# Moving the small stages of an attention and mixture-of-experts block to other half-steps of a hand-placed schedule

## The reference, cut to what matters

```python
q = (x @ Wq.T + bq) ...; k = ...; v = ...
q = _apply_rope(q, cos, sin); k = _apply_rope(k, cos, sin)
attn = softmax(einsum('bhsd,bhed->bhse', q, k) * scale)
x = x + (einsum('bhse,bhed->bhsd', attn, v) ... @ Wo.T + bo)
normed = rms_norm(layernorm(x).astype(bf16)) * norm_weight
scores, idx = top_k(normed @ gate_weight.T + gate_bias, 2); combine = softmax weights of the two
p1 = einsum('bsh,eoh->bseo', normed, mlp1_weight); act = g * sigmoid(1.702 * g) * (lin + 1)
x = x + xc + sum over e of combine[e] * (act @ mlp2_weight[e])
```

## Time and profile before

| | |
|---|---|
| median of 3 runs | 1128.25 us (1126.47 to 1128.8) |
| the profiled execution | 1125.54 us, of which the span from first to last instruction is 1123.7 us |
| PE busy | 953.0 us (85%), 5288 instructions |
| DVE busy | 822.6 us (73%), 1641 instructions |
| ACT busy | 694.7 us (62%), 905 instructions |
| POOL busy | 427.2 us (38%), 356 instructions |
| mean granted TensorE clock | 0.938 of full speed |

### The profile page before, as it was taken

The page is one execution under the profiler, slowest core; times in us unless marked ns, Lnnn a source line. Parts: engine busy times, 40 slices in busy tenths (PEclk is TensorE's granted clock), DMA queues, the critical chain, the costliest instruction groups (busy, mean ns, idle before and its releaser), DMA issues.

```text
span 1123.7 us, 16639 instructions
## 1 busy us (share of the span) xinstructions
PE 953.0 (85%) x5288; PEld 400.6 (36%) x5288; DVE 822.6 (73%) x1641; ACT 694.7 (62%) x905; POOL 427.2 (38%) x356
## 2 busy tenths in 40 slices
PE   4629999889888998989989898989999999995564
PEld 1302222234342443334442343324443443343343
DVE  5751211589968898589958898588968996997897
ACT  2317887766657675766658575766668777760231
POOL 2413302534364334543354434543342332333242
PEclk9868999999999999999999999999999999996686
DMA  5353434344545244444534244444534454331110
GB/s 162 97 120 69 114 82 115 81 104 110 114 90 137 72 105 109 109 101 103 124 82 117 82 108 106 104 91 114 124 82 114 105 123 97 89 91 38 42 57 24
DMA packets 79987, 109.81 MB, mean 98 GB/s; under 512 B 22530, under 2 KB 56722, under 8 KB 76818
## 3 DMA queue, kind: packets, MB, share of 16 engines
q1 hardware_dynamic: 61460, 83.47, 32.5%
q10 hardware_dynamic: 18432, 25.17, 7.7%
HBM read 82.90 MB, written 25.69 MB: 97 GB/s over the span
## 4 chain that ended last, share of the span: by engine, by line
PE 49%; DVE 27%; issue 8%; ACT 6%; POOL 3%; DMA 3%; SPq 2%; ACTq 0%; DVEq 0%; POOLq 0%
PE OP L698 14%; PE S L684 13%; PE D L670 7%; ACT probs L815 4%; DVE act_sb L1123 4%; DVE th_sb L1118 4%; DVE acc L1113 3%; PE A L653 3%; DVE l_sb L1103 3%; PE D L574 3%; DVE g_sb L1101 3%; PE BB L653 3%; PE D L596 3%; DMA o_scr<-O 1%; PE D L588 1%
## 5 line engine op out<-in xcount | busy, mean ns | idle before, releaser
L815 ACT ACTIVATE probs<-S 128x1024 f32<-128x1024 f32 x512 | 511.4, 1022 | 200.4 <-PE S L684 196.7
L684 PE MATMUL S<-Qs,Ks 98*128 98x512 bf16 x1024 | 304.2, 390 | 30.3 <-DMA Qs<-m_scr 15.2
L698 PE MATMUL OP<-probs,V 128*17 128x512 f32 x2048 | 276.4, 612 | 3.0 <-ACT O L824 3.0
L899 POOL TENSOR_TENSOR act_lo<-act_sb,act_hi 128x512 fp32r<-128x512 f32 x128 | 166.3, 1300 | 197.3 <-DVE act_hi L1129 160.8
L684 PEld LDWEIGHTS S<-Qs,Ks 98*128 98x128 bf16 x1024 | 80.3, 99 | 213.8 <-ACT probs L815 95.0
L670 PE MATMUL D<-W,act_hi 128*128 128x256 f32 x448 | 131.6, 326 | 14.0 <-DVE Vn L997 5.8
L1113 DVE SCALAR_TENSOR_TENSOR acc<-D,combh,acc 128x256 f32<-128x256 f32 x224 | 97.1, 475 | 45.8 <-PE D L670 45.6
L1118 DVE SCALAR_TENSOR_TENSOR th_sb<-th_sb,g_sb 128x512 f32<-128x512 f32 x128 | 126.8, 991 | 0.2
L893 POOL TENSOR_SCALAR W<-W2b 128x512 fp32r<-128x512 bf16 x64 | 46.1, 720 | 204.8 <-PE D L670 199.7
L670 PE MATMUL D<-W,act_lo 128*128 128x256 f32 x448 | 112.7, 284 | 0.0
L1123 DVE SCALAR_TENSOR_TENSOR act_sb<-l_sb,th_sb 128x512 f32<-128x512 f32 x128 | 106.0, 828 | 4.4
(11 more groups left out here) (138 smaller groups left out, 991.7 us busy)
## 6 DMA issues: line engine op xcount, KB each, us to landing
W<-in_w ACTq DMA_DIRECT2D x64, 256.0 KB, 2.9
Ks<-k_scr SPq DMA_DIRECT2D x32, 384.0 KB
W2b<-in_w ACTq DMA_DIRECT2D x64, 128.0 KB, 3.1
Ks<-k_scr SPq DMA_DIRECT2D x32, 256.0 KB
o_scr<-O SPq DMA_DIRECT2D x32, 256.0 KB, 4.7
q_scr<-parts SPq DMA_DIRECT2D x16, 384.0 KB, 3.5
k_scr<-parts SPq DMA_DIRECT2D x16, 384.0 KB, 2.5
Qs<-q_scr SPq DMA_DIRECT2D x32, 192.0 KB
```

The costliest lines, as they stand in the source:

```text
L684: last = mm(S[:, j2, C * i:C * (i + 1)], Ks[0:SROWS + MROWS, g % 2, j, P * kt:P * (kt + 1)], Qs[0:SROWS + MROWS, g % 2, j, :], start=True, ...
L698: last = mm(OP[32 * j:32 * j + VW, :], V[:, kt, HG * g + j, :], probs[:, s % 2, C * j:C * (j + 1)], start=kt == 0, stop=kt == KT - 1)
L815: nc.scalar.activation(probs[:, s % 2, 2 * C * j2:2 * C * (j2 + 1)], S[:, j2, :], ACT.Exp, scale=SCALE).then_inc(exp_done, 1)
L899: tt(act_lo[:, e % 2, it, :], act_sb[:, a % 2, :], act_hi[:, e % 2, it, :].bitcast(FP32), ALU.subtract).then_inc(lo_s, 1)
```

## The change

The table `AT` of places is rewritten, and `length` is split: POOL's subtraction becomes a stage `r1` of its own, five halves behind `qk` as it was, and `length` (PE and DVE) gets a place of its own for each block, as have `gmax`, `guard` and `flag`. No operation is added or taken out; only places, and with them the order in each engine's queue, change. In half-steps, before and after:

| stage | before | after |
|---|---|---|
| x_next | 8 | 10 |
| xT1 | 8 | 9 |
| qk0, qk1, qk2, qk3 | 10, 12, 22, 30 | 19, 21, 30, 34 |
| rope, part1, r1, part2, part3 (behind qk) | +2, +3, +5, +7, +10 | the same |
| length0 to length3 | 15, 17, 27, 35 | 24, 26, 35, 41 |
| v0, v1 | 37, 42 | 43, 49 |
| gmax, guard, flag | 36, 39, 41 | 42, 45, 47 |
| wo1 | 14 | 15 |
| stats2, rstd2, xc | 15, 16, 17 | 16, 17, 18 |
| ss, ms, rrms | 18, 18, 20 | 19, 20, 21 |
| nf, nfT | 22, 24 | 23, 25 |
| logits, gates1, etop, gates2 | 26, 26, 27, 28 | 27, 27, 28, 29 |
| combT, b20, b21 | 32, 33, 34 | 31, 33, 36 |

```diff
-    AT = {"x_next": 8, "stats1": 1, "rstd1": 1, "xn": 4, "xT0": 7, "xT1": 8, "qk0": 10, "qk1": 12, "qk2": 22,
-          "qk3": 30, "rope": 2, "part1": 3, "length": 5, "part2": 7, "part3": 10, "v0": 37, "v1": 42, "gmax": 1,
-          "guard": 4, "flag": 6, "x1_in": 0, "x1_b": 11, "wo0": 13, "wo1": 14, "stats2": 15, "rstd2": 16, "xc": 17, "ss":
-          18, "ms": 18, "rrms": 20, "nf": 22, "nfT": 24, "logits": 26, "gates1": 26, "etop": 27, "gates2": 28,
-          "combT": 32, "b20": 33, "b21": 34}
+    AT = {"x_next": 10, "stats1": 1, "rstd1": 1, "xn": 4, "xT0": 7, "xT1": 9, "qk0": 19, "qk1": 21, "qk2": 30, "qk3":
+          34, "rope": 2, "part1": 3, "r1": 5, "part2": 7, "part3": 10, "length0": 24, "length1": 26,
+          "length2": 35, "length3": 41, "v0": 43, "v1": 49, "gmax": 42, "guard": 45, "flag": 47, "x1_in": 0,
+          "x1_b": 11, "wo0": 13, "wo1": 15, "stats2": 16, "rstd2": 17, "xc": 18, "ss": 19, "ms": 20, "rrms":
+          21, "nf": 23, "nfT": 25, "logits": 27, "gates1": 27, "etop": 28, "gates2": 29, "combT": 31, "b20":
+          33, "b21": 36}
...
         place(PREP, h, ("qk", a))
-        for st in ("rope", "part1", "length", "part2", "part3"):
+        place(PREP, AT[f"length{a}"], ("length", a))
+        for st in ("rope", "part1", "r1", "part2", "part3"):
             place(PREP, h + AT[st], (st, a))
     for st in ("gmax", "guard", "flag"):
-        place(PREP, h + AT["length"] + AT[st], (st, 0))
+        place(PREP, AT[st], (st, 0))
...
-            HEAD += [("length", *tile[2]), ("part2", *tile[2]), ("part3", *tile[2])]
+            HEAD += [("r1", *tile[2]), ("length", *tile[2]), ("part2", *tile[2]), ("part3", *tile[2])]
...
-                elif st == "length":
+                elif st == "r1":
                     pool.wait_ge(qk_p1, 4 * u + a + 1)
                     tt(sw[:, a % 2, :], rot[:, a % 2, :], parts[:, a % 2, 0, :], ALU.subtract).then_inc(qk_r1, 1)
```

## The result

The changed kernel takes 1225.75 us (median of 4 runs, 1213.64 to 1228.42) beside 1128.53 us for the kernel before (4 runs): a ratio of 1.0845 (95% interval 1.0769 to 1.0920), 97 us slower. Slower was forecast, but by 24 us and not by 97, and the time lies far above the range. The profiled execution took 1223.82 us with a span of 1222.0 us, 98.3 more than the span before. In the code after, the lines named in the front have two added (L574 is L576, L1113 is L1115).

A forecast was written before the change was run, and what follows sets the result against it. No engine alone: ACT bounds steps 10 to 13, PE and DVE near limit in 14 to 25. Per full window -7.6 + 7.8 + 4.8 = +5.0, four times; window 1 +5.3, tail -1: +24, 1150 us, range 1110 to 1170.

The forecast's parts named there:

- Steps 4 to 9 (-7.6): Two qk products, length0, length1 and their waits leave: 33.8 to 26.2 us per full window, bounds -8.5 and -6.5.
- the 2.9 foretold: Steps 5 and 6 of window 3 should each be shorter by 2.9 us, with no wait for acc.
- the 1.7 foretold: Steps 8 and 9: length0 and length1, with the waits of the down behind them, leave, saving 1.7 us.
- two exchanges that were put at nothing: xT1 ahead of step 5's down, wo1 ahead of step 8's: each makes and saves a wait, together nothing.
- Steps 10 to 13 (+7.8): The first two blocks' chain to length1, woven with POST's norm, takes 19.4 us for 11.6; bounds +6.1 and +10.
- Steps 14 to 25 (+4.8): 2.8 us of added DVE work plus two of four POOL collisions at 1.0 each; bounds -2 and +7.
- two added waits: up 1 waits for g_sb behind 14 small DVE operations; qk3 waits for b20's copy; both counted inside +4.8.
- the gain at `wo1` and `b21` stands against `gates1`: Windows 6 and 7, POST alone: gain and loss offset, so put at nothing.
- the gain foretold for `final`: Tail: final of window 6 runs ahead of ms on DVE while ACT does ss, about -1 us.
- (a): Rival: PE bounds steps 14 to 25 and bank waits go, so faster, 1107 us; chance 0.19.
- (b): Rival: long PE waits bring a lower clock, +7.5 to +15 us more, 1157 to 1165 us; chance 0.25.
- (c): Rival: steps 4 to 13 cancel and steps 14 to 25 hide what comes, 1126 us; chance 0.08.

The follow-up runs named there:

- e1: Changed kernel with POST (wo1 to b21) back at its old places, so PREP's moves alone; 1185.2 us, ratio 1.0532.
- e2: Kernel before with all of POST (wo1 to b21) at its new places and nothing else moved; 1188.0 us, ratio 1.0545.
- e11: Changed kernel with qk1 at half-step 26 for 21 and length1 at 32 for 26; 1236.4 us, ratio 1.0983.
- e12: Changed kernel with length0 at half-step 23 for 24, so its maximum stands ahead of nf on DVE; 1227.6 us, ratio 1.0903.
- e6: Kernel before with qk2, qk3 and their followers (length2, length3, v0, v1, gmax, guard, flag) at their new half-steps; 1163.4 us, ratio 1.0343.
- e3: Changed kernel with logits, gates1, etop and gates2 back at half-steps 26, 26, 27, 28; 1202.7 us, ratio 1.0678.
- e4: Changed kernel with qk0, qk1, length0 and length1 and what follows them back at their old half-steps; 1210.9 us, ratio 1.0747.
- e10: Changed kernel with extra overwritten products on PE, two before combT's wait and three ahead of nfT's bank wait; 1220.3 us, ratio 1.0823.
- e8: Changed kernel with combT at half-step 33 for 31 and b20 at 34 for 33; 1229.4 us, ratio 1.0877.
- e13: Changed kernel with length3 at half-step 42 for 41; 1225.3 us, ratio 1.0838.
- e15: Kernel before with b21 alone moved, to half-step 36 for 34; 1136.1 us, ratio 1.0074.

## Why the prediction was wrong, and where it held

**Steps 4 to 9 (-7.6).** Right in the mechanism: -6.4 on the mean of the four full windows, just outside the upper bound of -6.5. The `qk`'s wait for `acc` is gone as foretold; step 6 of window 3 went from 5.86 to 2.93 us, the 2.9 foretold. Step 5 went from 5.86 to 4.48 only (4.02 in the other full windows): the product of `xT1` now falls into it, and in those three its `down` waits 0.35 us for the copy. `wo1`, moved ahead of the `down` of step 8, lengthened that step from 3.76 to 5.43 and shortened step 7 from 6.19 to 3.77; steps 7 to 9 together gave 1.5 us on the mean, of the 1.7 foretold. So of the two exchanges that were put at nothing, that of `xT1` costs most of the difference.

**Steps 10 to 13 (+7.8).** A chain came, as foretold, but it was too short in size: +10.1, at the bound of +10. Of the signs foretold, ACT waits for POOL's sum, 2.6 us in window 3's steps 10 to 13, and `length1` for ACT's copy of `nfT`, but 1.1 us only. PREP's part alone gives +7.8 (e1; `nf` is at 935 ns there), the size forecast for the whole. POST's part alone gives +0.3 (e2), so 2 us come only where the two meet: what was mis-sized is the weaving with POST. Collisions of DVE and POOL were priced for steps 14 to 25 and not here, where `nf` now runs beside `rope1`, at 3.7 us more in four passes. The rows had shown the same of another operation. The rule of the Trainium skill that the forecast weighed there (page SBUF — State Buffer, section Who interferes with whom) covers `nf` too, which has two inputs in SBUF, and the trace agrees with it: each `nf` lasts about one POOL pass. That the collision, rather than the length of PREP's chain beside POST, sets the end of the stretch is not shown; e11 takes both away, and in e12 `nf` falls to 962 ns with the stretch unchanged.

**Steps 14 to 25 (+4.8): the step that failed.** Measured +10.4, over the bound of +7. The forecast named two added waits and wrote that "both are DVE time and are inside the +4.8". They are not. It priced them as work of one busy engine, and the engine was not the bound: its work grew by 3.4 us in window 3 and its gaps by 8.5. The rest went into waits in a ring: PE waits for a DVE operation that queues behind others, the scores and with them ACT's exponentials and `tanh` queue behind PE, and DVE then waits for ACT (6.5 us in window 3). Two parts that the forecast had at nothing, or inside that work, make it:

- The late blocks (`qk2` "beside it", `length3`, `v`), +6.5 per full window (e6 less before, on the fastest of its four runs).
- The gates in the second half of step 13: putting them back takes 6.4 of the 6.7 us away by which C of window 6 grew, and 2.2 us of C in the full windows (e3). POST's moves without PREP's cost 8.0 us there (e2), but with the two waits that the change doesn't have; what they cost in the change beyond the gates is not shown. This is also the sentence on windows 6 and 7, "the gain at `wo1` and `b21` stands against `gates1`": measured +8.0 and +6.2 us in these two windows.

The part that the forecast did price here, the pair's DVE work, is the small one: e1's C is 2.6 us over e6's, and putting the pair back takes 0.4 away (e4), which is within what the windows differ among themselves. The parts measured by themselves don't add up: 2.6, 6.5 and 8.0 would be 17, and the change shows 10.4.

**The sum.** Over the profiled executions the eight windows and the tail give, against the forecast: windows 2 to 5 +60.7 (+20), window 1 +15.7 (+5.3), windows 6 and 7 +14.2 (0), window 0 +3.5 (0), the tail +4.2 (-1); together 98.3 for 24. Of the 74 us that were missed, 46 lie in steps 14 to 25 of all windows, 15 in steps 10 to 13, 10 in steps outside the three stretches, where nothing was put, and 5 in the tail; steps 4 to 9 gave 2 us more than foretold, since window 0, at nothing in the forecast, gained 7.2 there (and lost 8.5 behind). In the tail the gain foretold for `final` did not show; with the gates back (e3) the tail is 0.7 us shorter than before. One slip besides: +24 on the median shown is 1152.5, not 1150.

**The rivals.** (a), PE the bound and the stretch shrinking, is refuted: it grew most. That DVE is not the bound is borne out, but PE is not it either: with the clock raised at two waits (e10) the time falls by 5.5 us only. (b), the lower clock, happened, 0.904 for 0.938, and is a small share: with the mean clock given back 92 of the 97 us remain, or 90 of 104 by the far ends of the two intervals. In the kernel after, the two full windows with the lower clock in C are 3 us longer there than the other two; if the clock made all of that, it would be 15 us in five windows. The rule of the Trainium skill cited for it (page TensorE: Matmul & The Clock Gate, section HAM oscillation — how this bites in real kernels) describes most of these rows: the values behind `combT`'s waits of 2.0 to 2.5 us took 1.6 to 1.9 us for 1.05 in six of seven windows. In window 5 they took 1.05 behind a wait of 2.3, so not every wait paid; and what the low clock costs falls in part into time in which PE would wait. (c) is out.

**What stays open.** How the growth of C divides among its waits can't be read from mending them singly, since they replace one another, and a version with all of them gone was not found. Nor is it shown why the two parts of the change overlap by 20 us; the 26.4 us of waits in e2 at neighbours that the change parts again (5.7 are left) would be enough, but no run takes them out of e2.

## What to carry to other kernels

Before a stage is moved off a crowded place, look up what its result has behind it on the next engine's queue: in this schedule gates that stood half a step later on DVE held up an expert's take-up and cost 6.4 us in a window without PREP and 2.2 in the others, more than a bank conflict that the moves ended (1 us for `qk`, 1.8 for `b21`). Two engines that are both near 90% busy in a stretch are not each other's cover; price a wait added there as lost for everything that stands behind it on three queues, and distrust a sum that books it as work inside one of them. And one mended wait proves nothing until the stretch is shorter: in e8 and e13 the wait came back at the next user of the bank, and in e15 `b21` waited for another one before it. The same holds for half a change tried alone: e2 made neighbours, and waits, that the whole change doesn't have.

## What the runs showed of the hardware

A bf16 operation of 128x256 on DVE with two inputs in SBUF went from 469 ns to 1.40 us each, four in a row, beside POOL's passes over 128x512 of 1.26 to 1.47 us, and to 1122 ns on the mean of all. In proportion to its length alone that is more than the f32 `th_sb` of the earlier trace rows paid, 0.68 to 1.68 us: the short operation lasts about one POOL pass. And the granted clock rose from 0.904 to 0.934 with five extra products per window, while the time hardly followed: 1225.8 to 1220.3 us.
